# Expert slots loaded already turned: rows with their halves apart, a transposing DMA, and the weighting of results on ScalarE

## What is computed

```python
router_logits = x @ gate_w.T                       # x: 2048 tokens of 256, 16 experts
topk_w, topk_idx = jax.lax.top_k(softmax(router_logits), 4)
topk_w = topk_w / topk_w.sum(axis=-1, keepdims=True)
shared = _silu_mul(x @ shared_gate_up.T, 704) @ shared_down.T * sigmoid(x @ shared_gate_vec.T)
def step(acc, ew):                                 # one of the 16 experts
    w_gu, w_d, cw = ew
    h = _silu_mul(x @ w_gu.T, 176)
    return (acc + h @ w_d.T * cw[:, None], None)
```

## Time and profile before

| | us |
|---|---|
| runs, median of 3 | 956.32 |
| runs, lowest and highest | 954.98, 961.11 |
| the profiled execution's span | 957.6 |
| PE busy in it | 919.9 |
| DVE busy | 771.4 |
| POOL busy | 505.0 |
| ACT busy | 439.1 |

### The profile page before, as it was taken

One profiled execution on the slowest core, in us unless ns is written; L12 is line 12 of the kernel. 1 busy time (PEld: TensorE's weight loads), 2 busy tenths in 40 slices (PEclk: granted clock), 3 DMA queues, 4 the chain that ended last, 5 costly groups with the idle time before them and its releaser, 6 DMA issues.

```text
span 957.6 us, 19531 instructions
## 1 busy us (share of the span) xinstructions
PE 919.9 (96%) x6337; PEld 825.6 (86%) x6337; DVE 771.4 (81%) x1704; ACT 439.1 (46%) x1227; POOL 505.0 (53%) x380
## 2 busy tenths in 40 slices
PE   6899999999999999999999999989999999999996
PEld 6789898989899888989888898877887799999985
DVE  6978877977887989877798976765778888888857
ACT  3656745454434654333564333472245444444430
POOL 1453424465453435777453677624626377777760
PEclk9999999999999999999999999998999999999998
DMA  7786389899156952303793231325151277787769
GB/s 267 260 339 238 131 305 388 313 393 364 53 181 246 400 191 105 111 24 117 287 373 115 88 112 48 122 65 237 52 216 69 75 126 130 129 132 129 125 109 314
DMA packets 75586, 179.09 MB, mean 187 GB/s; under 512 B 7777, under 2 KB 42465, under 8 KB 74465
## 3 DMA queue, kind: packets, MB, share of 16 engines
q1 hardware_dynamic: 61040, 158.80, 46.0%
q0 software_dynamic: 14448, 19.05, 12.2%
HBM read 98.35 MB, written 79.47 MB: 186 GB/s over the span
## 4 chain that ended last, share of the span: by engine, by line
PE 76%; DVE 8%; issue 6%; DMA 3%; POOL 3%; ACT 2%; SPq 1%; another core or an unknown queue 0%; DVEq 0%; POOLq 0%; ACTq 0%
PE bank L550 11%; PE bank L552 10%; PE bank L551 10%; PE bank L852 6%; PE bank L630 6%; PE bank L954 3%; POOL xs L1350 3%; PE bank L830 3%; PE bank L616 3%; PE bank L832 3%; PE bank L834 3%; PE bank L656 3%; PE bank L658 2%; PE bank L657 2%; DVE turn L1514 2%
## 5 line engine op out<-in xcount | busy, mean ns | idle before, releaser
L1310 POOL TENSOR_TENSOR z_lo<-prob_t,z_hi 128x512 fp32r<-128x512 f32 x64 | 82.5, 1296 | 191.3 <-ACT z_hi L1197 167.6
L1514 DVE SCALAR_TENSOR_TENSOR turn<-bank,bqk,trig 128x1024 f32<-128x1024 f32 x128 | 160.6, 1277 | 23.3 <-PE bank L552 20.8
L1342 POOL TENSOR_TENSOR rot<-turn 128x512 f32<-128x512 f32 x64 | 101.8, 1591 | 107.4 <-DVE turn L1514 91.9
L1403 POOL DMA_INDIRECT sums<-ysb,token_at x79 | 123.3, 1561 | 57.0 <-DMA sums<-ysb,token_at 26.4
L550 PE MATMUL bank<-xt_hi,w_hi 128*128 128x512 f32 x256 | 105.4, 412 | 3.1 <-DVE xt_lo L1478 1.7
L1183 ACT COPY prob_t<-bank 128x512 f32<-128x512 f32 x64 | 37.5, 586 | 150.9 <-PE bank L616 142.7
L1142 ACT ACTIVATE prob<-prob,negmax 128x128 f32<-128x128 f32 x256 | 99.1, 389 | 2.5 <-DVE negmax L1499 2.4
L552 PE MATMUL bank<-xt_hi,w_lo 128*128 128x512 f32 x256 | 100.0, 391 | 0.0
L551 PE MATMUL bank<-xt_lo,w_hi 128*128 128x512 f32 x256 | 99.7, 390 | 0.0
L1350 POOL DMA_INDIRECT xs<-xh,dest x64 | 71.8, 1122 | 41.9 <-issue 38.3
L1153 ACT COPY v<-bank 128x512 f32<-128x512 f32 x64 | 37.6, 588 | 119.7 <-PE bank L552 118.6
(11 more groups left out here) (201 smaller groups left out, 2663.9 us busy)
## 6 DMA issues: line engine op xcount, KB each, us to landing
xs<-zeros SPq DMA_DIRECT2D x16, 2120.0 KB, 15.6
w_hi<-w_dram SPq DMA_DIRECT2D x24, 768.0 KB, 10.0
w_lo<-w_dram SPq DMA_DIRECT2D x24, 768.0 KB, 9.4
xe_all<-xs SPq DMA_DIRECT2D x79, 132.5 KB
wo_hi<-wo_dram SPq DMA_DIRECT2D x26, 256.0 KB, 9.6
wo_lo<-wo_dram SPq DMA_DIRECT2D x26, 256.0 KB, 11.1
sums<-zeros SPq DMA_DIRECT2D x3, 2176.0 KB, 13.0
raw<-in_wqkv SPq DMA_DIRECT2D x16, 384.0 KB, 4.4
```

The costliest lines, as they stand in the source:

```text
L1342: nc.gpsimd.tensor_tensor(rot[m][1][:], turn[m][1], turn[m][2], ALU.add).then_inc(rot_pool, 1)
L1403: nc.gpsimd.indirect_dma_start(sums_dram[s % SUMS], bass.IndirectOffsetOnAxis(ap=token_at[:, s:s + 1], axis=0), ysb[s % YBUFS][:], None, c ...
L1514: last = nc.vector.scalar_tensor_tensor(turn_all[m][:, 2 * i:2 * i + 2, :], qk_bank[2 * m + i][:].unsqueeze(1).to_broadcast([128, 2, GT]), ...
```

## The change

The rows of `xs` become 288 words: they are seen as two planes of 288 sixteen-bit halves. The first holds the low halves of the 256 values, then the numbers, weights and the token's number (9 words from word META = 128); the second holds the high halves. SP's load of a slot is now two transfers: a transposing DMA of 256 half rows of 256 halves each, which leaves in `xe[s % 4]` the 256x128 words turned, and a plain one of the nine words into `xe_meta[s % 4]`. `slot_transpose` is gone from PE; `slot_high` and `slot_low` read `xe` in SBUF instead of a bank. SP issues the load of slot s + 4 when `slot_low` and `slot_ids` of slot s are done.

To fill such rows, the tokens are normalised into `xn` (the last group into `again`), and ACT copies the halves apart into `xh` (`split_rows`, 2048 halves a partition, four times in all); `scatter` waits for that too. The second normalising of group 1 (`tokens_again(1)`) moves behind the routing of the last group, since `again` is now in use before.

`slot_out` moves from DVE to ACT: an activation with the function Copy and `found` as scale, placed behind `slot_turned_take(s - 1)`.

```diff
 PARTS = 4
-XW = D + 2 * TOPK + 1
-TOKEN_AT = D + 2 * TOPK
+META = D // 2
+METAS = 2 * TOPK + 1
+PLANE = META + 16
+XW = 2 * PLANE
+TOKEN_AT = META + 2 * TOPK
...
         gctx = ExitStack()
-        xe_all = sb("xe_all", [128, 4, XW], c=gctx)
-        xe = [xe_all[:, i, :] for i in range(4)]
+        xe = [sb(f"xe{i}", [128, CH, 128], c=gctx) for i in range(4)]
+        xe_meta = [sb(f"xe_meta{i}", [128, METAS], c=gctx) for i in range(4)]
...
             sp.wait_ge(table_ready, 1)
-            def slot_rows(s):
-                return bass.ds(sp.value_load(table[1:2, s:s + 1], min_val=0, max_val=ROWS - 128), 128)
+            planes = rows_dram.bitcast(U16).rearrange("r (h c) -> (r h) c", h=2)
...
-                sp.dma_start(xe[s % 4][:], rows_dram[slot_rows(s), :]).then_inc(xe_loaded[s % 4], 16)
+                at = sp.value_load(table[1:2, s:s + 1], min_val=0, max_val=ROWS - 128)
+                sp.dma_start_transpose(xe[s % 4][:].bitcast(U16),
+                                       planes[bass.ds(at * 2, 2 * 128), 0:D]).then_inc(xe_loaded[s % 4], 16)
+                sp.dma_start(xe_meta[s % 4][:].bitcast(U32), rows_dram[bass.ds(at, 128), META:META + METAS]).then_inc(xe_loaded[s % 4], 16)
...
-                sp.wait_ge(et_ready, s + 1)
+                sp.wait_ge(eh_lo_done, s + 1)
...
                     for b in range(GB):
-                        src = xh[:, b, c * 128:(c + 1) * 128] if routed else again[:, b, c * 128:(c + 1) * 128]
-                        last = nc.tensor.transpose(banks[c][:, b * 128:(b + 1) * 128], src, ident[:])
+                        src = xn if routed and g < GROUPS - 1 else again
+                        last = nc.tensor.transpose(banks[c][:, b * 128:(b + 1) * 128],
+                                                   src[:, b, c * 128:(c + 1) * 128], ident[:])
...
                 last.then_inc(hm_used, 1)
-            def slot_transpose(s):
-                pe.wait_ge(xe_loaded[s % 4], 16 * (s // 4 + 1))
-                if s >= 2:
-                    pe.wait_ge(eh_lo_done, s - 1)
-                for c in range(CH):
-                    last = nc.tensor.transpose(banks[s % 2][:, c * 128:(c + 1) * 128],
-                                               xe[s % 4][:, c * 128:(c + 1) * 128], ident[:])
-                last.then_inc(et_ready, 1)
...
             pe.wait_ge(table_ready, 1)
-            pe.wait_ge(spread_taken, 1)
-            slot_transpose(0)
-            slot_transpose(1)
...
                     experts[(s + 1) % 4] = slot_expert(s + 1)
-                if s + 2 < SLOTS:
-                    slot_transpose(s + 2)
...
+
+            def split_rows(g):
+                act.wait_ge(xh_ready, GB * (g + 1))
+                if g:
+                    act.wait_ge(scattered[g - 1], 16 * GB * TOPK)
+                else:
+                    act.wait_ge(run_zero, 1)
+                src = xn if g < GROUPS - 1 else again
+                nc.scalar.copy(xh[:].bitcast(U16).rearrange("p b (h c) -> p b h c", h=2)[:, :, :, 0:D],
+                               src[:].bitcast(U16).rearrange("p b (c h) -> p b h c", h=2)).then_inc(xh_split, 1)
...
                     shared_silu(0, 1)
+                    split_rows(2)
...
                             out_hi(q)
+                if p == 1 and 1 < g < GROUPS:
+                    split_rows(g - 2)
...
             tokens_high(4)
+            split_rows(GROUPS - 1)
...
             def slot_high(s):
-                act.wait_ge(et_ready, s + 1)
+                act.wait_ge(xe_loaded[s % 4], 2 * 16 * (s // 4 + 1))
...
-                nc.scalar.copy(xe_hi[s % 2][:], banks[s % 2][:, 0:D].rearrange("p (c t) -> p c t", c=CH)).then_inc(eh_hi_done, 1)
+                nc.scalar.copy(xe_hi[s % 2][:], xe[s % 4][:]).then_inc(eh_hi_done, 1)
...
                 nc.scalar.copy(eht[s % 2][:], banks[4 + s % 2][:, 0:128]).then_inc(eht_taken, 1)
+            def slot_out(s):
+                act.wait_ge(ey_ready, s + 1)
+                act.wait_ge(id_ready, s + 1)
+                if s >= YBUFS:
+                    act.wait_ge(y_stored[(s - YBUFS) % SUMS], 16 * ((s - YBUFS) // SUMS + 1))
+                nc.scalar.activation(ysb[s % YBUFS][:], banks[6 + s % 2][:, 0:D], ACT.Copy,
+                                     scale=found[:, s:s + 1]).then_inc(ey_taken, 1)
...
-            for s in range(SLOTS + 1):
+            for s in range(SLOTS + 2):
...
-                if s >= 1:
+                if 1 <= s <= SLOTS:
...
+                if s >= 2:
+                    slot_out(s - 2)
...
                 pool.wait_ge(dest_ready, g + 1)
+                pool.wait_ge(xh_split, g + 1)
...
-                        rows_dram, bass.IndirectOffsetOnAxis(ap=dest[:, at:at + 1], axis=0), xh[:, n // TOPK, :], None
+                        rows_dram, bass.IndirectOffsetOnAxis(ap=dest[:, at:at + 1], axis=0),
+                        xh[:, n // TOPK, :].bitcast(U32), None
...
                     dve.wait_ge(vt_ready, 2 * h)
+                    dve.wait_ge(xh_split, h)
...
                 stepped(nc.vector.tensor_copy(topf[:], topi[:]))
-                nc.vector.tensor_copy(xh[:, :, D:D + TOPK], topf[:, :, 0:TOPK])
+                if g:
+                    dve.wait_ge(scattered[g - 1], 16 * GB * TOPK)
+                nc.vector.tensor_copy(xh[:, :, META:META + TOPK], topf[:, :, 0:TOPK])
...
                 token_roots(g * GB, (g + 1) * GB)
-                if g:
-                    dve.wait_ge(scattered[g - 1], 16 * GB * TOPK)
+                if g < GROUPS - 1:
+                    dve.wait_ge(vt_ready, 2 * (g + 1))
+                else:
+                    dve.wait_ge(tt_ready, CH * 3)
+                dst = xn if g < GROUPS - 1 else again
...
-                    normalise(xh[:, b, 0:D], g * GB + b, xh_ready)
+                    normalise(dst[:, b, :], g * GB + b, xh_ready)
...
-                    dve.wait_ge(tt_ready, CH * 3)
+                    dve.wait_ge(tt_ready, CH * 5)
+                    dve.wait_ge(xh_split, GROUPS)
...
                 if g == 1 and p == 1:
+                    nc.vector.memset(xh[:, :, META + METAS:PLANE], 0.0)
+                    nc.vector.memset(xh[:, :, PLANE + META:XW], 0.0)
...
             shared_mult(1, 2)
-            tokens_again(1)
...
             counts_take()
+            tokens_again(1)
...
                     dve.wait_ge(eup_ready, s - 1)
-                nc.vector.tensor_tensor(xe_lo[s % 2][:], banks[s % 2][:, 0:D].rearrange("p (c t) -> p c t", c=CH),
-                                        xe_hi[s % 2][:].bitcast(F32), ALU.subtract).then_inc(eh_lo_done, 1)
+                nc.vector.tensor_tensor(xe_lo[s % 2][:], xe[s % 4][:], xe_hi[s % 2][:].bitcast(F32),
+                                        ALU.subtract).then_inc(eh_lo_done, 1)
...
                 nc.vector.tensor_tensor(eh[s % 2][:, 192:192 + IREST], up[:, 128:INTER], h[:, 128:INTER], ALU.mult).then_inc(eh_done, 1)
-            def slot_out(s):
-                dve.wait_ge(ey_ready, s + 1)
-                if s >= YBUFS:
-                    dve.wait_ge(y_stored[(s - YBUFS) % SUMS], 16 * ((s - YBUFS) // SUMS + 1))
-                dve.wait_ge(id_ready, s + 1)
-                nc.vector.tensor_scalar(ysb[s % YBUFS][:], banks[6 + s % 2][:, 0:D], found[:, s:s + 1], None,
-                                        ALU.mult).then_inc(ey_taken, 1)
...
             def slot_ids(s):
-                dve.wait_ge(xe_loaded[s % 4], 16 * (s // 4 + 1))
-                nc.vector.scalar_tensor_tensor(match[:, s % 2], xe[s % 4][:, D:D + TOPK], slot_e[:, s:s + 1],
-                                               xe[s % 4][:, D + TOPK:TOKEN_AT], ALU.is_equal, ALU.mult).then_inc(matched, 1)
-                nc.vector.tensor_scalar(token_at[:, s:s + 1], xe[s % 4][:, TOKEN_AT:TOKEN_AT + 1], FAR, spare_id,
+                dve.wait_ge(xe_loaded[s % 4], 2 * 16 * (s // 4 + 1))
+                m = xe_meta[s % 4]
+                nc.vector.scalar_tensor_tensor(match[:, s % 2], m[:, 0:TOPK], slot_e[:, s:s + 1],
+                                               m[:, TOPK:2 * TOPK], ALU.is_equal, ALU.mult).then_inc(matched, 1)
+                nc.vector.tensor_scalar(token_at[:, s:s + 1], m[:, 2 * TOPK:METAS], FAR, spare_id,
...
             shared_add(2)
-            for s in range(SLOTS + 2):
+            for s in range(SLOTS + 1):
...
-                if s >= 2:
-                    slot_out(s - 2)
-                if 1 <= s <= SLOTS:
+                if s >= 1:
...

```

More of the change, by code:

```diff
@@ L89 @@
 I32 = mybir.dt.int32
+U16 = mybir.dt.uint16
 BF16 = mybir.dt.bfloat16
@@ L95, in decoder @@
             count_in, route_in, out):
-    rows_dram = nc.dram_tensor("xs", (ROWS, XW), F32, kind="Internal").ap()
+    rows_dram = nc.dram_tensor("xs", (ROWS, XW), U32, kind="Internal").ap()
     sums_dram = [nc.dram_tensor(f"sums{i}", (TOKENS + 128, D), F32, kind="Internal").ap() for i in range(SUMS)]
@@ L336, in decoder @@
         xh_ready = sem("xh_ready")
+        xh_split = sem("xh_split")
```

(7 more changed lines are left out.)

## The result

The changed kernel takes 1015.3 us (median of 4 runs, 1014.5 to 1017.0) where the kernel before takes 955.7 us: a ratio of 1.059, interval 1.055 to 1.063. Forecast were 944 us and a range that ended at 1000. A second measurement of the same pair gave 1.052 (1.048 to 1.056), so the loss is 50 to 60 us. It lies in the loop over the expert slots, and SP, the engine that only issues transfers, sets the pace there.

What follows compares the result with a forecast made beforehand. PE was taken as the bound, 96% busy. The expert loop gives 77 x (2.06 - 1.90) = 12.3 us, all else 0: 957.6 becomes 945.3, less 1.3 for the runs' median 944.0 us; range 939 to 1000.

Steps and rivals of the forecast that it cites:

- Issue on SP: Slot loads in the expert loop: SP needs 1.11 us before, 1.61 to 1.81 after, under POOL's 1.86; upper bound 2.91.
- SP's issue: Expert loop: transposing transfer holds SP as long as the slowest fill, 2.91 us a slot, 65 slower, 1022 us; chance 0.09.
- The 390 against 1309 ns: Turning a 128x128 block on TensorE against transposing DMA; four blocks in series would be 5.24 us a slot, 1201 in all.
- Turns off PE: Expert loop: PE goes from 2.06 to 1.85 us a slot, POOL's 1.86 takes over, 15.4 us off if nothing else is late.
- The ring and the landings: Three result buffers in the expert loop: late scatter landings give 1.86 to 2.07 us a slot; 1.90 taken, 12.3 us gained.
- The engines' share: Transfer engines in the expert loop: scatters 1.17 plus loads 0.7 us of all sixteen, 1.87 a slot, level with POOL's floor.
- The engines run full: Expert loop: transfers priced by packets need 2.37 us a slot, 24 us slower, 980; at the scatters' price 1080; chance 0.22.
- Weighting on ScalarE: Expert loop: ACT rises by 0.37 to 1.39 of 1.86 us, DVE falls from 1.84 to 1.36; no effect on time.
- Ahead of the loop: Between POOL's last scatter and the first product: bounds 1.7 us gained to 2 us lost, taken as 0.
- Splits and fills: Before the expert loop: four ACT splits of 2.1 us each and zero fills 9% larger, hidden or uncounted, taken as 0.
- PE waiting for the expert input in most slots, with SP busy back to back: Expert loop: sign that the prediction is wrong because the load is too slow, through the time its issue holds SP.

Runs made afterwards that it cites:

- the version that relieves SP: Changed kernel with the small transfer issued by ScalarE's queue and the slot address's bounds test left away on both queues: 954.7 us, ratio 0.998.
- the version with four buffers: Changed kernel with small transfer on ScalarE's queue, no bounds test, rows of 276 words, four result buffers instead of three: 954.7 us, ratio 0.995.

## Why the prediction was wrong

**The step that failed** is the term "Issue on SP" in the cost of the load. It took the transposing transfer's issue between 0.34 us (as the plain one) and 0.535 (the median fill), and kept 1.64, the slowest fill, as an upper bound with "a single extreme" against it. Measured: 1.21 us in the median and never under 0.91, and nearly the same for half of the data and for half as much again. The second transfer was put at 0.5 us and cost 0.64 to 0.74 (from 2.72 and 2.83, the two executions of the changed kernel, to 2.09 in the run without it): 0.43 of issue, 0.08 of address arithmetic, the rest pauses and slow instances. With the measured values the prediction's own sum, 1.11 - 0.34 + 1.21 + 0.64 to 0.74, gives 2.62 to 2.72 us a slot, and the median distance in the trace is 2.64 from one transposing issue to the next, 2.70 from one address load to the next. The mean of 2.83 lies above because single instructions take up to 2.58 us.

**The rival "SP's issue"** was the right mechanism, with the right mark (it decides from 0.79 us for the transposing issue) and almost the right time: 1022 us against 1015. That closeness is partly luck: its 1.64 us for the issue was too high (1.28 in the mean) and its 0.5 for the second transfer too low. It had 0.09 of the chance and lay outside the range. The choice between the two ends was made by likeness, "near the plain load because the bytes are the same", though no row showed a transposing issue and 0.79 lay inside the two bounds, 0.34 and 1.64. With bounds on both sides of the deciding point and nothing to place the value between them, a third or more of the chance belonged there, and the range had to reach it.

**The 390 against 1309 ns** of the Trainium skill ("VectorE: DVE Perf Modes", the three transpose paths) warned in the right direction, but not by its sum of 1201 us: four blocks in series didn't occur, since in the version that relieves SP a whole transposing load came every 2.03 us, under half of 5.24. Its 390 ns, given for a block of bf16, the prediction compared with two overlapping blocks at 0.38 us; one 128x128 block of float32 takes 0.27 us here. The Trainium skill's "Perfetto Trace Analysis", the section on DMA instructions issued in hardware, says what the profile's row of such an instruction spans: the sequencer's time while descriptors are made, not the movement of the data. That is how the 1.21 us are to be read, and the run with half the bytes agrees (1.13 us).

**The other steps.** *Turns off PE*, 0.20 us a slot: right in kind. With the plain load the gap was 1.95 us instead of 2.03, and the time 0.8% lower, where the sum had 1.90 and 1.3%. *The ring and the landings*: right in kind, shown only in the relieved version, where the fourth buffer is worth 0.08 us a slot; in the changed kernel nothing waited for it. *The engines' share*: the loads' queue was put at 0.7 us of all sixteen a slot. The transfer queues of the changed kernel in its loop (packets, MB, share of 16 engines):

```profile
q0 software_dynamic: 10327, 9.41, 41.7%
q1 hardware_dynamic: 49605, 9.79, 29.6%
```

Over the 205 us from 770 to 975, or 205 / 2.83 = 72 slots, that is 0.84 us for the loads (q1) and 1.19 for the scatters (q0), which the prediction had at 1.17. The loads come in some 685 packets a slot, where the prediction counted 384, of 0.020 us each instead of 0.050. So "The engines run full" was nearer than the central value said, but the mark by which it would decide, packet times adding up to the slot's 2.06 us, doesn't hold: with four buffers they add up to 1.15 x 1.96 = 2.25 us in a slot of 1.96. *Weighting on ScalarE*, nothing: right, shown in the kernel before (0.999) and in the relieved version (954.7 against 954.6 us); it takes 0.49 us there, where the prediction had 0.37. *Ahead of the loop*, 0 with 2 us either way: the first load is issued 2.9 us earlier in one execution and 2.9 later in another of the same kernel (750.4 and 756.2 against 753.3), more than the term was worth. *Splits and fills*, nothing: these same first loads, one earlier and one later, show no loss ahead of the loop. One sum is off by 2 us: 1.94 us a slot gives 947 us, and the range's 949 only with the 2 us that the head might lose.

**What the signs said.** The prediction's last part asked for SP's new issue under 0.6 us, and named "PE waiting for the expert input in most slots, with SP busy back to back" as the sign of the issue's price. The trace shows that, with ScalarE as the one that waits for the input (116.5 us) and TensorE behind it.

## What to carry to other kernels

An engine that only issues transfers has a time budget per turn of a loop like any other: add up all its instructions, address loads and pauses included, and take the price of a new kind of instruction as open until a row of that kind has been seen. Where the deciding point lies between the two bounds, the chance belongs to it, however harmless the nearest known row looks. When several small costs stand on one queue, moving any one of them off can give back almost all that was lost, and it shows at once where the next limit is.

## What the runs showed of the hardware

- A transposing transfer holds SP 1.13, 1.21 and 1.24 us for 128, 256 and 384 columns of 256 half rows; a plain one of 256 pieces 0.39, a small plain one of 128 pieces of 36 B 0.33 to 0.43, one of 16 B 0.25.
- Reading one word from SBUF into a register of SP takes 0.27 us, and 0.53 behind a row of five issues; why is open.
- ScalarE's queue issued a plain transfer in 0.35 us while an instruction of ScalarE was still running.
- The profile's share of the 16 DMA engines can pass 1: it was 1.15 in the version with four buffers.
- TensorE's clock fell in the changed kernel where a late load had left it idle. SP's transposing issue at 845.90 took 2.16 us, the input landed late, and after 2.72 us with no matmul TensorE worked at a granted 0.50, that is 1.2 GHz (columns as in the earlier trace rows):

```profile
849.73 1.21 PE L952 MATMUL bank<-dne,eht 128*128 x2 [2.72 <-ACT eht L1294]
```

```profile
848.00:849.70 1.70, 0.00 (x0) 0.00 (x0) 0.41 (x2) 0.84 (x4) 0.00 (x0) 0.99 1.00 84
849.70:852.50 2.80, 2.77 (x10) 2.59 (x11) 1.95 (x12) 1.54 (x6) 1.56 (x1) 0.50 0.25 49
```

  The two down products took 1.21 us there, and 0.69 at the full clock (at 844.75). From 763.10 to 911.00 the clock was 0.98, so this adds little; it costs extra just where a slot is already late.
